# A gated recurrence on one core: the unbounded gathers of the first four tiles bring two layers of gates instead of one

## The chip, the cores and the metric

The kernel runs on one core of one Trainium2 chip. The metric is the device time of one execution in microseconds (us). The engines are PE (TensorE), DVE (VectorE), ACT (ScalarE), POOL (GpSimd) and SP (SyncE, which here only issues DMAs).

## The reference

2048 rows of 256 numbers pass six layers. In each, the row's token picks one row of a gate table with 4000 rows:

```python
def _L0_rec_ref(state, token, ih, hh):
    n_layers = ih.shape[0]                 # 6
    for i in range(n_layers):
        gate = ih[i][token]                # ih: 6 x 4000 x 256
        state = jnp.tanh(state + jnp.matmul(state, hh[i]) * gate)   # hh: 6 x 256 x 256
    return state
```

The tokens are drawn from 49 to 31985, so about seven in eight lie beyond the table, and for them the last row of the table is what the reference reads. All is float32.

## The kernel before

**Tiling.** The 2048 rows are 16 tiles of 128, taken in 8 pairs q. `order` lists 48 steps (layer, pair), all pairs of layer 0 first, then all of layer 1, and so on; every engine runs a program written out by hand in this order, and semaphores tie the engines together.

**One step.** PE multiplies the pair's state (as columns) by the layer's weights: in layer 0 in float32 (line 288), in later layers as three float16 products of a head and a rest (line 296). DVE multiplies the product by the gates into `sums` (`gated`, lines 465 and 468); the old state is added by DVE (line 480, all of layer 0) or POOL (line 280); ACT takes the tanh (line 403). For the next layer the new state has to be split and turned: for even pairs PE turns it (line 328), then ACT and DVE make head and rest (lines 385 and 485); for odd pairs ACT and DVE make head and rest of the rows (lines 391 and 492) and SP issues a DMA transpose (line 233). In layer 0 the old rows of pairs 1 to 7 come from PE too (line 336). Weights are scaled by powers of two that come out of column sums (`w_sums`, `totals` at line 345, `scales`); the totals for layers 2 to 5 stand in PE's program right after the first product of layer 1 and wait for the last addition of layer 0.

**Gates.** `gates` holds, for every tile, six layers of 256 numbers for each of its 128 rows. POOL fills it by indirect DMAs, one after another (the gathers), in two ways:

- For tiles 0 to 3 (`FIRST`), an unbounded gather brings layer 0 alone from `gate_first`, a table whose last row stands 128 times so that all tokens beyond the end find one (line 263). It waits for nothing but the index.
- A bounded gather skips the indices beyond the table. Its destination is filled beforehand with the table's last row, by an ACT or DVE copy from `last_rows` (`fill`, lines 367 and 430). Tiles 4 to 15 get all six layers in this way (line 273), then tiles 0 to 3 get layers 1 to 5 from `gate_later` (line 270).

POOL issues the four unbounded gathers, then the bounded ones of tiles 4 to 15, then those of tiles 0 to 3. `first_in[q]` and `gates_in[q]` count what has landed. DVE waits for `first_in` (q 0 and 1) or `gates_in` (q 2 to 7) ahead of the gating in layer 0, and for `gates_in` of q 0 and 1 ahead of their gating in layer 1.

**Loads.** SP loads the token, `last_rows` (768 KB), then for each pair the state's columns (line 204, 256 KB) and, between them, the weights of each layer (line 211, 256 KB) and the rows of pair 0 (line 208). From pair 2 on a load waits until the load two pairs earlier has landed.

Of the kernel before, what the change touches and what calls it, by code (L numbers as in the profile page):

```python
# [5 lines left out]
def gated_recurrence(nc, token, state_cols, state_rows, weights, gate_first, gate_later, gate_rows, gate_last, out):  # L6
# [18 lines left out]
    PAIR = 2  # L25
    PAIRS = TILES // PAIR
    LAST = LAYERS - 1
    SPLIT = LAYERS - 1

    order = [(l, q) for l in range(LAYERS) for q in range(PAIRS)]  # L30
# [4 lines left out]

    DMA_PAIRS = (1, 3, 5, 7)
    PE_INSTEAD = ()

    TURN_LAG = 3
    HEAD_LAG, HEAD_ROWS_LAG = 3, 1  # L40
# [6 lines left out]


    FIRST = (0, 1, 2, 3)
    GATHERS = (4, 5, 6, 7, 8, 9, 10, 11, 12, 13, 14, 15, 0, 1, 2, 3)  # L50
    ACT_FILLS = {-1: (5, 7, 10, 12, 14, 0, 1), 1: (2,)}
    DVE_FILLS = {-1: (4, 6, 8, 9, 11, 13), 0: (15,), 2: (3,)}
# [21 lines left out]
    PRODUCTS, TURNED, COPIES = 3, 2, 2  # L74

    def by_dma(i):
        return order[i][0] < LAST and order[i][1] in DMA_PAIRS and order[i] not in PE_INSTEAD

    def by_pe(i):
        return order[i][0] < LAST and not by_dma(i)  # L80
# [25 lines left out]
    with ExitStack() as ctx:  # L106
        def sb(name, shape, dt):
            return ctx.enter_context(nc.sbuf_tensor(name, shape, dt))
# [4 lines left out]
        def sem(name):  # L113
            return ctx.enter_context(nc.semaphore(name))
# [5 lines left out]
        gates = sb("gates", [P, TILES, LAYERS, HID], fp32)  # L120
# [32 lines left out]
        first_in = [sem(f"first_in{q}") for q in range(PAIRS)]  # L153
# [28 lines left out]
        def pair_rows(t, q):  # L182
            return t[:, PAIR * q:PAIR * (q + 1), :]
# [63 lines left out]
        @block.gpsimd  # L247
        def _(pool):
            nc.gpsimd.iota(limit[:, :], pattern=[[0, 1]], base=VOCAB - 1, channel_multiplier=1).then_inc(limit_ready, 1)
            nc.gpsimd.memset(ident[:, :], 0.0).then_inc(ident_zero, 1)  # L250
            pool.wait_ge(ident_zero, 1)
            nc.gpsimd.affine_select(out=ident[:, :], in_=ident[:, :], compare_op=ALU.not_equal, fill=1.0,
                                    base=0, pattern=[[-1, P]], channel_multiplier=1).then_inc(ident_ready, 1)

            pool.wait_ge(index_steps, INDEX_STEPS)
            by_act = [t for tiles in ACT_FILLS.values() for t in tiles]
            by_vector = [t for tiles in DVE_FILLS.values() for t in tiles]

            def offset(t):
                return bass.IndirectOffsetOnAxis(ap=index[:, t:t + 1], axis=0)  # L260

            for t in FIRST:
                pool.indirect_dma_start(gates[:, t, 0, :], None, gate_first, offset(t)).then_inc(first_in[t // PAIR], 16)  # L263
            for t in GATHERS:
                if t in by_act:
                    pool.wait_ge(act_filled, by_act.index(t) + 1)
                else:
                    pool.wait_ge(vector_filled, by_vector.index(t) + 1)
                if t in FIRST:
                    pool.indirect_dma_start(gates[:, t, 1:, :].rearrange("p l h -> p (l h)"), None, gate_later, offset(t),  # L270
                                            bounds_check=VOCAB - 1, oob_is_err=False).then_inc(gates_in[t // PAIR], 16)
                else:
                    pool.indirect_dma_start(gates[:, t].rearrange("p l h -> p (l h)"), None, gate_rows, offset(t),  # L273
                                            bounds_check=VOCAB - 1, oob_is_err=False).then_inc(gates_in[t // PAIR], 16)

            for i in range(STEPS):
                if on_pool(i):
                    q = order[i][1]
                    pool.wait_ge(gated_ready, i + 1)
                    nc.gpsimd.tensor_tensor(sums[:, q], sums[:, q], pair_rows(state, q),  # L280
                                            ALU.add).then_inc(pool_added, 1)
# [80 lines left out]
        @block.scalar  # L362
        def _(act):
            def fill(t):
                act.wait_ge(last_in, 16)
                lo = 1 if t in FIRST else 0
                nc.scalar.activation(gates[:, t, lo:, :].rearrange("p l h -> p (l h)"), last_rows[:, lo * HID:],  # L367
                                     ACT.Copy).then_inc(act_filled, 1)

            def w_sums(l):  # L370
                act.wait_ge(w_in[1 + l], 16)
                if l >= 1:
                    act.wait_ge(w_sum_ready, l)
                nc.scalar.activation(w_abs[:, :], w_full[:, 1 + l, :], ACT.Abs,
                                     accum_out=w_sum[:, l:l + 1]).then_inc(w_sum_ready, 1)

            def w_make_head(l):
                act.wait_ge(scale_steps, (1 if l == 0 else 2) * SCALE_STEPS)
                nc.scalar.activation(w_head[:, l, :], w_full[:, 1 + l, :], ACT.Copy,  # L379
                                     scale=w_up[:, :].bitcast(fp32)[:, l:l + 1]).then_inc(w_head_ready, 1)  # L380

            def make_head(i):
                q = order[i][1]
                act.wait_ge(turned_ready, pe_turns(i))
                nc.scalar.activation(split_cols[:, q, 0], turned_bank(i)[:, :, :, :], ACT.Copy,  # L385
                                     scale=STATE_SCALE).then_inc(head_ready, 1)

            def make_head_rows(i):
                q = order[i][1]
                act.wait_ge(copy_ready, dma_turns(i))  # L390
                nc.scalar.activation(split_rows[:, q, 0], copy_bank(i)[:, :, :], ACT.Copy,  # L391
                                     scale=STATE_SCALE).then_inc(head_rows_ready, 1)

            def new_state(i):
                q = order[i][1]
                if on_pool(i):
                    act.wait_ge(pool_added, pool_adds(i))
                else:
                    act.wait_ge(vector_added, vector_adds(i))
                for n, cut in enumerate(cuts(i)):  # L400
                    if n >= 1:
                        act.wait_ge(vector_added, vector_adds(i) + n)
                    nc.scalar.activation(pair_rows(state, q)[:, cut], sums[:, q, cut], ACT.Tanh).then_inc(state_ready, 1)  # L403
                if by_dma(i):
                    if dma_turns(i) > COPIES:
                        act.wait_ge(rest_rows_ready, dma_turns(i) - COPIES)
                    nc.scalar.activation(copy_bank(i)[:, :, :], sums[:, q], ACT.Tanh).then_inc(copy_ready, 1)  # L407

            for t in ACT_FILLS[-1]:
                fill(t)  # L410
            for i in range(STEPS):
                if i >= HEAD_LAG and by_pe(i - HEAD_LAG):
                    make_head(i - HEAD_LAG)
                if i >= HEAD_ROWS_LAG and by_dma(i - HEAD_ROWS_LAG):
                    make_head_rows(i - HEAD_ROWS_LAG)
                new_state(i)
                for t in ACT_FILLS.get(i, ()):
                    fill(t)
                if i in SUMS_AT:
                    w_sums(SUMS_AT[i])  # L420
                if i in HEADS_AT:
                    w_make_head(HEADS_AT[i])
# [3 lines left out]
        def _(dve):  # L426
            def fill(t):
                dve.wait_ge(last_in, 16)
                lo = 1 if t in FIRST else 0
                nc.vector.tensor_copy(gates[:, t, lo:, :].rearrange("p l h -> p (l h)"),  # L430
                                      last_rows[:, lo * HID:]).then_inc(vector_filled, 1)

# [22 lines left out]
            def gated(i, n, cut):  # L455
                layer, q = order[i]
                dve.wait_ge(product_ready, i + 1 + n)
                if layer == 0:
                    dve.wait_ge(first_in[q] if PAIR * q in FIRST else gates_in[q], 16 * PAIR)
                elif layer == 1 and PAIR * q in FIRST:  # L460
                    dve.wait_ge(gates_in[q], 16 * PAIR)
                product = product_bank(i, cut)[:, cut]
                g = pair_rows(gates, q)[:, cut, layer, :]
                if layer == 0:
                    nc.vector.tensor_tensor(sums[:, q, cut], product, g, ALU.mult).then_inc(gated_ready, 1)  # L465
                else:
                    down = w_down[:, :].bitcast(fp32)[:, layer - 1:layer]
                    nc.vector.scalar_tensor_tensor(out=sums[:, q, cut], in0=product, scalar=down, in1=g,  # L468
                                                   op0=ALU.mult, op1=ALU.mult).then_inc(gated_ready, 1)
# [96 lines left out]
```

## Time and profile before

| | us |
|---|---|
| median of 3 runs | 102.38 (102.11 to 102.92) |
| the profiled execution | 102.9 |
| its span in the trace | 101.1 |
| PE / DVE / ACT / POOL busy | 86.9 / 80.1 / 77.5 / 68.2 |

The span is what the engines' records cover; 1.8 us of the profiled execution lie around it. A busy share is an average over a load stage with layer 0, a dense middle and a tail, whose limits differ. Times in the trace count from the span's start.

### The profile page before, as it was taken

The page shows a single profiled execution, that of the slowest core. Times are in us where ns is not written, and L with a number is a line of the kernel's source. Part 1 is how long each engine was busy: PE and PEld are TensorE (multiplying, and loading weights), DVE is VectorE, ACT ScalarE, POOL GpSimd, SP SyncE. Part 2 cuts the span into 40 slices and gives each one's busy share as a digit, 9 for nine tenths or more (in the row PEclk, how much of TensorE's full clock was granted, in tenths as well). Part 3 has the DMA queues.
Part 4 walks back from the last instruction along what each step waited for, and adds up shares of the span by engine and source line. Part 5 has one row for each costly group of instructions (what it writes and reads, how often), then busy time and mean ns, then how long its engine had stood idle before and what let it go on. Part 6 is the DMA issues. An engine that isn't in the chain of part 4 may idle for free.

```text
span 101.1 us, 1829 instructions
## 1 busy us (share of the span) xinstructions
PE 86.9 (86%) x664; PEld 76.0 (75%) x664; DVE 80.1 (79%) x128; ACT 77.5 (77%) x133; POOL 68.2 (67%) x63
## 2 busy tenths in 40 slices
PE   5209999969995299999999999999999999999910
PEld 5108588948883277999999999999999999988800
DVE  1159966697660775789999899998999999989990
ACT  5059999799871266789699998999989978992641
POOL 3578787777772045477698868987499949879000
PEclk9999999999999655999999999999999999999995
DMA  1899899953999405057255551544545425964984
GB/s 23 286 338 392 258 280 314 334 186 96 70 107 169 53 3 110 0 104 59 52 104 102 104 104 35 112 82 90 104 60 121 81 55 104 96 118 82 367 310 174
DMA packets 27368, 14.25 MB, mean 141 GB/s; under 512 B 23772, under 2 KB 24028, under 8 KB 27360
## 3 DMA queue, kind: packets, MB, share of 16 engines
q1 hardware_dynamic: 24864, 12.07, 52.1%
q0 software_dynamic: 2496, 2.07, 10.1%
q8 instruction: 5, 0.08, 0.3%
q14 instruction: 3, 0.02, 0.1%
HBM read 17.31 MB, written 2.10 MB: 192 GB/s over the span
## 4 chain that ended last, share of the span: by engine, by line
PE 55%; DVE 17%; DMA 13%; issue 7%; POOL 6%; ACT 0%; SPq 0%; DVEq 0%; POOLq 0%
PE products L296 46%; DMA gates<-in_gate_rows,index 8%; PE turned L328 8%; DVE gates L430 6%; POOL gates L273 6%; DMA last_rows<-in_gate_last 5%; DVE sums L468 4%; DVE sums L480 4%; DVE split_cols L485 1%; DVE sums L465 1%; DVE split_rows L492 1%; PE spare L345 1%; ACT state L403 0%; SPq L225 0%; POOLq L273 0%
## 5 line engine op out<-in xcount | busy, mean ns | idle before, releaser
L296 PE MATMUL products<-w_head,split_cols 128*128 128x256 f16 x316 | 57.1, 279 | 0.0
L280 POOL TENSOR_TENSOR sums<-sums,state 128x512 f32<-128x512 f32 x36 | 45.6, 1272 | 16.9 <-DVE sums L468 16.5
L296 PE MATMUL products<-w_rest,split_cols 128*128 128x256 f16 x158 | 44.1, 279 | 0.0
L403 ACT ACTIVATE state<-sums 128x512 f32<-128x512 f32 (+1 forms) x49 | 30.4, 619 | 15.2 <-DVE sums L480 7.3
L296 PEld LDWEIGHTS products<-w_head,split_cols 128*128 128x128 f16 x316 | 31.9, 101 | 4.0
L468 DVE SCALAR_TENSOR_TENSOR sums<-products,w_down,gates 128x512 f32<-128x512 f32 (+1 forms) x40 | 29.5, 738 | 4.8 <-PE products L296 4.8
L288 PE MATMUL products<-w_full,first_cols 128*128 128x256 f32 x64 | 18.0, 430 | 4.6 <-DMA w_full<-in_weights 4.4
L288 PEld LDWEIGHTS products<-w_full,first_cols 128*128 128x128 f32 x64 | 13.3, 218 | 7.4 <-issue 4.7
L296 PEld LDWEIGHTS products<-w_rest,split_cols 128*128 128x128 f16 x158 | 15.8, 100 | 2.1
L273 POOL DMA_INDIRECT gates<-in_gate_rows,index x12 | 13.2, 1097 | 3.7 <-issue 3.4
L367 ACT ACTIVATE gates<-last_rows 128x1536 f32<-128x1536 f32 (+1 forms) x8 | 10.6, 1390 | 4.1 <-DMA last_rows<-in_gate_last 4.1
L485 DVE SCALAR_TENSOR_TENSOR split_cols<-turned,split_cols 128x512 f16<-128x512 f32 x20 | 13.6, 679 | 0.0
L492 DVE SCALAR_TENSOR_TENSOR split_rows<-copies,split_rows 128x512 f16<-128x512 f32 x20 | 13.6, 679 | 0.0
L328 PE MATMUL turned<-ident,state 128*128 128x128 f32 x80 | 12.5, 280 | 0.0
L391 ACT ACTIVATE split_rows<-copies 128x512 f16<-128x512 f32 x20 | 11.8, 590 | 0.4
L385 ACT ACTIVATE split_cols<-turned 128x512 f16<-128x512 f32 x20 | 11.7, 585 | 0.1
L407 ACT ACTIVATE copies<-sums 128x512 f32<-128x512 f32 x20 | 11.7, 587 | 0.0
L465 DVE TENSOR_TENSOR sums<-products,gates 128x512 f32<-128x512 f32 x8 | 5.5, 688 | 6.4 <-DMA gates<-in_gate_rows,index 4.2
L328 PEld LDWEIGHTS turned<-ident,state 128*128 128x128 f32 x80 | 9.9, 146 | 0.4
L430 DVE COPY gates<-last_rows 128x1536 f32<-128x1536 f32 (+1 forms) x8 | 7.2, 946 | 3.1 <-DMA last_rows<-in_gate_last 3.1
L451 DVE SCALAR_TENSOR_TENSOR w_rest<-w_full,w_up,w_head 128x512 f16<-128x512 f32 x5 | 6.3, 1257 | 0.8 <-ACT w_head L379 0.8
L263 POOL DMA_INDIRECT gates<-in_gate_first,index x4 | 4.7, 1178 | 2.6 <-DVE index L507 1.7
(37 smaller groups left out, 40.0 us busy)
## 6 DMA issues: line engine op xcount, KB each, us to landing
first_cols<-in_state_cols SPq DMA_DIRECT2D x8, 256.0 KB, 4.1
out<-state SPq DMA_DIRECT2D x7, 256.0 KB, 2.4
w_full<-in_weights SPq DMA_DIRECT2D x6, 256.0 KB, 5.4
last_rows<-in_gate_last SPq DMA_DIRECT2D x1, 768.0 KB, 4.9
split_cols<-split_rows SPq DMA_TRANSPOSE x20, 3.0
state<-in_state_rows SPq DMA_DIRECT2D x1, 256.0 KB, 6.2
out<-state SPq DMA_DIRECT2D x2, 128.0 KB, 1.7
gates<-in_gate_rows,index POOLq DMA_INDIRECT x12, 4.8
```

The lines of the kernel that those rows point to most:

```text
L273: pool.indirect_dma_start(gates[:, t].rearrange("p l h -> p (l h)"), None, gate_rows, offset(t), bounds_check=VOCAB - 1, oob_is_err=False) ...
L280: nc.gpsimd.tensor_tensor(sums[:, q], sums[:, q], pair_rows(state, q), ALU.add).then_inc(pool_added, 1)
L288: last = nc.tensor.matmul(bank[:, j, :], first_cols[:, q, k, j * P:(j + 1) * P], w_full[:, 0, k * HID:(k + 1) * HID], start=(k == 0), stop ...
L296: last = nc.tensor.matmul(bank[:, j, :], split_cols[:, q, s, j, k, :], w[:, l - 1, k * HID:(k + 1) * HID], start=(n == 0), stop=(n == len( ...
L328: last = nc.tensor.transpose(turned_bank(i)[:, j, k, :], state[:, PAIR * q + j, k * P:(k + 1) * P], ident[:, :])
L385: nc.scalar.activation(split_cols[:, q, 0], turned_bank(i)[:, :, :, :], ACT.Copy, scale=STATE_SCALE).then_inc(head_ready, 1)
L391: nc.scalar.activation(split_rows[:, q, 0], copy_bank(i)[:, :, :], ACT.Copy, scale=STATE_SCALE).then_inc(head_rows_ready, 1)
L403: nc.scalar.activation(pair_rows(state, q)[:, cut], sums[:, q, cut], ACT.Tanh).then_inc(state_ready, 1)
L430: nc.vector.tensor_copy(gates[:, t, lo:, :].rearrange("p l h -> p (l h)"), last_rows[:, lo * HID:]).then_inc(vector_filled, 1)
L468: nc.vector.scalar_tensor_tensor(out=sums[:, q, cut], in0=product, scalar=down, in1=g, op0=ALU.mult, op1=ALU.mult).then_inc(gated_ready, 1)
L485: nc.vector.scalar_tensor_tensor(out=split_cols[:, q, 1], in0=turned_bank(i)[:, :, :, :], scalar=STATE_SCALE, in1=split_cols[:, q, 0], op0 ...
L492: nc.vector.scalar_tensor_tensor(out=split_rows[:, q, 1], in0=copy_bank(i)[:, :, :], scalar=STATE_SCALE, in1=split_rows[:, q, 0], op0=ALU. ...
```

## The change

The unbounded gathers of tiles 0 to 3 bring layers 0 and 1, 2 KB a row instead of 1 KB, from a `gate_first` of twice the width. The fills and the bounded gathers of these four tiles begin at layer 2, four layers instead of five. DVE waits for the bounded gathers of q 0 and 1 ahead of layer 2 instead of layer 1. `DMA_INSTEAD` is an empty tuple, so the new `by_dma` picks the same steps as before.

```diff
@@ FIRST
     FIRST = (0, 1, 2, 3)
+    FIRST_LAYERS = 2
@@ by_dma
-        return order[i][0] < LAST and order[i][1] in DMA_PAIRS and order[i] not in PE_INSTEAD
+        layer, q = order[i]
+        return layer < LAST and (q in DMA_PAIRS and (layer, q) not in PE_INSTEAD or (layer, q) in DMA_INSTEAD)
@@ POOL
             for t in FIRST:
-                pool.indirect_dma_start(gates[:, t, 0, :], None, gate_first, offset(t)).then_inc(first_in[t // PAIR], 16)
+                pool.indirect_dma_start(gates[:, t, :FIRST_LAYERS, :].rearrange("p l h -> p (l h)"), None, gate_first,
+                                        offset(t)).then_inc(first_in[t // PAIR], 16)
...
                 if t in FIRST:
-                    pool.indirect_dma_start(gates[:, t, 1:, :].rearrange("p l h -> p (l h)"), None, gate_later, offset(t),
+                    pool.indirect_dma_start(gates[:, t, FIRST_LAYERS:, :].rearrange("p l h -> p (l h)"), None, gate_later, offset(t),
                                             bounds_check=VOCAB - 1, oob_is_err=False).then_inc(gates_in[t // PAIR], 16)
@@ fill, on ACT and on DVE
-                lo = 1 if t in FIRST else 0
+                lo = FIRST_LAYERS if t in FIRST else 0
@@ gated, on DVE
-                elif layer == 1 and PAIR * q in FIRST:
+                elif layer == FIRST_LAYERS and PAIR * q in FIRST:
                     dve.wait_ge(gates_in[q], 16 * PAIR)
@@ host
-    gate_first = _np.concatenate([gate_rows[:, :hid], _np.repeat(gate_rows[-1:, :hid], 127, axis=0)])
+    gate_first = _np.concatenate([gate_rows[:, :2 * hid], _np.repeat(gate_rows[-1:, :2 * hid], 127, axis=0)])
...
-        "gate_later": gate_rows[:, hid:],
+        "gate_later": gate_rows[:, 2 * hid:],
```

No instruction changes its place on its engine; what changes is the wait on two of DVE's. Here is DVE's program from the last gating of layer 0 to the second of layer 1, before:

```order
L465 TENSOR_TENSOR sums<-products,gates 128x512 [waits gates_in7,product_ready]
L485 SCALAR_TENSOR_TENSOR split_cols<-turned,split_cols 128x512 [waits head_ready]
L480 TENSOR_TENSOR sums<-sums,spare 128x512 [waits rows_turned,gated_ready]
L437 TENSOR_SCALAR w_total<-spare 128x4 [waits total_ready]
L440 TENSOR_SCALAR w_expo<-w_total 128x4 [waits scale_steps]
L443 TENSOR_SCALAR w_up<-w_expo 128x4 [waits scale_steps]
L446 TENSOR_SCALAR w_down<-w_expo 128x4
L468 SCALAR_TENSOR_TENSOR sums<-products,w_down,gates 128x512 [waits gates_in0,product_ready]
L492 SCALAR_TENSOR_TENSOR split_rows<-copies,split_rows 128x512 [waits head_rows_ready]
L468 SCALAR_TENSOR_TENSOR sums<-products,w_down,gates 128x512 [waits gates_in1,product_ready]
```

And the same stretch of DVE after the change:

```order
L469 TENSOR_TENSOR sums<-products,gates 128x512 [waits gates_in7,product_ready]
L489 SCALAR_TENSOR_TENSOR split_cols<-turned,split_cols 128x512 [waits head_ready]
L484 TENSOR_TENSOR sums<-sums,spare 128x512 [waits rows_turned,gated_ready]
L441 TENSOR_SCALAR w_total<-spare 128x4 [waits total_ready]
L444 TENSOR_SCALAR w_expo<-w_total 128x4 [waits scale_steps]
L447 TENSOR_SCALAR w_up<-w_expo 128x4 [waits scale_steps]
L450 TENSOR_SCALAR w_down<-w_expo 128x4
L472 SCALAR_TENSOR_TENSOR sums<-products,w_down,gates 128x512 [waits product_ready]
L496 SCALAR_TENSOR_TENSOR split_rows<-copies,split_rows 128x512 [waits head_rows_ready]
L472 SCALAR_TENSOR_TENSOR sums<-products,w_down,gates 128x512 [waits product_ready]
```

The waits for `gates_in0` and `gates_in1` have moved eight steps down, to the first two gatings of layer 2; that for `gates_in7`, the last of layer 0, stays.

## Rows read from the trace of the kernel before

**Rows 1.** The chain that ended last: start us, us, what:
```profile
24.74 7.93 DMA gates<-in_gate_rows,index
...
34.69 0.59 PE spare L345 x2
35.28 2.58 PE products L296 x12
37.87 0.85 PE turned L328 x4
38.72 3.59 PE products L296 x24
42.31 0.44 PE turned L328 x4
42.75 2.62 PE products L296 x24
...
88.60 1.32 PE products L296 x12
```

**Rows 2.** DVE in order of time: start us, us, what, idle before and releaser:
```profile
11.34 0.68 DVE L465 TENSOR_TENSOR sums<-products,gates 128x512 f32<-128x512 f32 x1
...
14.39 0.69 DVE L465 TENSOR_TENSOR sums<-products,gates 128x512 f32<-128x512 f32 x1 [0.78 <-PE products L288]
...
17.89 0.89 DVE L430 COPY gates<-last_rows 128x1280 f32<-128x1280 f32 x1
...
32.76 0.69 DVE L465 TENSOR_TENSOR sums<-products,gates 128x512 f32<-128x512 f32 x1 [3.34 <-DMA gates<-in_gate_rows,index]
...
35.88 0.74 DVE L468 SCALAR_TENSOR_TENSOR sums<-products,w_down,gates 128x512 f32<-128x512 f32 x1
...
37.90 0.75 DVE L468 SCALAR_TENSOR_TENSOR sums<-products,w_down,gates 128x512 f32<-128x512 f32 x1 [0.68 <-PE products L296]
```

**Rows 3.** Waits from 0 to 36 us: total us, times, longest:
```profile
PE spare L345 <- DVE sums L480: 3.0, 1, 3.0
...
PE spare L336 <- DVE sums L480: 0.9, 1, 0.9
...
PE products L288 <- DMA first_cols<-in_state_cols: 0.2, 1, 0.2
```

**Rows 4.** The page's 40 slices of the span (2.53 us each), granted clock in tenths:
```profile
PEclk9999999999999655999999999999999999999995
```

**Rows 5.** POOL in order of time:
```profile
7.48 1.44 POOL L263 DMA_INDIRECT gates<-in_gate_first,index  x1 [0.30 <-issue]
...
17.93 0.99 POOL L273 DMA_INDIRECT gates<-in_gate_rows,index  x1 [0.30 <-issue]
...
27.33 0.99 POOL L270 DMA_INDIRECT gates<-in_gate_later,index  x1 [0.30 <-issue]
...
29.93 0.99 POOL L270 DMA_INDIRECT gates<-in_gate_later,index  x1 [0.30 <-issue]
```

**Rows 6.** DMA, us to landing: the gathers issued at 27.33 and at 29.93:
```profile
gates<-in_gate_later,index POOLq DMA_INDIRECT x1, 6.3
...
gates<-in_gate_later,index POOLq DMA_INDIRECT x1, 4.7
```

**Rows 7.** Stretches of 2 us: stretch, PE, PEld, DVE, ACT, POOL busy, clock, DMA share, GB/s:
```profile
8.00:10.00 2.00, 2.00 (x6) 1.55 (x6) 2.00 (x3) 2.00 (x2) 1.70 (x2) 1.00 1.05 406
10.00:12.00 2.00, 1.78 (x5) 0.97 (x4) 2.00 (x3) 2.00 (x3) 1.70 (x2) 1.00 0.95 307
...
22.00:24.00 2.00, 1.64 (x10) 1.52 (x11) 2.00 (x4) 1.96 (x5) 1.55 (x2) 1.00 0.30 80
```

**Rows 8.** Groups by line and form, 0 to 36 us: busy us, mean ns, idle before:
```profile
L367 ACT ACTIVATE gates<-last_rows 128x1280 f32<-128x1280 f32 x3 | 3.7, 1255 | 0.0
```

**Rows 9.** DMA transposes, us to landing: the one issued at 23.5 us, then the median of all:
```profile
split_cols<-split_rows SPq DMA_TRANSPOSE x1, 8.9
...
split_cols<-split_rows SPq DMA_TRANSPOSE x20, 3.0
```

More of the change, by code:

```diff
@@ L37, in gated_recurrence @@
     PE_INSTEAD = ()
+    DMA_INSTEAD = ()
     TURN_LAG = 3
@@ L428, in fill @@
                 dve.wait_ge(last_in, 16)
-                lo = 1 if t in FIRST else 0
+                lo = FIRST_LAYERS if t in FIRST else 0
                 nc.vector.tensor_copy(gates[:, t, lo:, :].rearrange("p l h -> p (l h)"),
```

## The prediction

> **What bounds the kernel now.** I read the chain of waits first. From 34.69 us to the last product at 88.60 it is nothing but PE: 24 products of 2.62 us and a turn of 0.44 us, over and over [rows 1]. Nothing that frees DVE, ACT or POOL there gives time. Ahead of that block stands one transfer: the gather issued at 24.74, in flight for 7.93 us, landed at 32.66 [rows 1]. It is the twelfth bounded gather, tile 15, and the order of POOL's program says so: four unbounded ones, then tiles 4 to 15. DVE's program shows who needs it. The last gating of layer 0, pair 7, starts at 32.76 after 3.34 us of idleness that this gather ended [rows 2]. Its addition releases the totals at line 345, for which PE sat idle 3.0 us [rows 3]. So layer 0 ends when tile 15's gates land, and all else in layer 0 has some 3 us to spare.
>
> The idleness costs a second time. The granted clock falls from full to half (2.4 to 1.2 GHz) in slices 14 to 16, roughly 33 to 40 us [rows 4], behind the 3.0 us in which PE did nothing. Twelve products, a turn and 24 products take 2.58 + 0.85 + 3.59 = 7.02 us there; at the later rate they are 1.32 + 0.44 + 2.62 = 4.38 us [rows 1]. The low clock costs 2.6 us.
>
> The question is therefore narrow: does the change move the landing of tile 15's gates, or the idleness of PE before it?
>
> **The wait that is taken out.** The gatings of pairs 0 and 1 in layer 1 no longer wait for the bounded gathers of tiles 0 to 3. These were issued at 27.33 (tile 1, the last of pair 0) and 29.93 (tile 3, the last of pair 1) [rows 5] and needed 6.3 and 4.7 us to land [rows 6]: 33.6 and 34.6. The gatings started at 35.88, straight behind the scales, and at 37.90, after 0.68 us of waiting for PE's products [rows 2]. Both gathers were there 2.3 and 3.3 us earlier. The removed wait was worth nothing: 0 us. It would only be worth something if the rest of layer 0 ended over 2 us earlier, and it ends on tile 15, whose gather stands ahead of these in the same queue.
>
> **The bytes that are added.** Each unbounded gather brings 128 rows of 1 KB more; four of them 4 x 128 x 1024 = 0.52 MB. They fall where the DMA engines are full: 406 GB/s at a share of 1.05 from 8 to 10 us, 307 GB/s at 0.95 from 10 to 12 us [rows 7]. The extra transfer takes 0.52 MB / 406 = 1.3 us to 0.52 / 307 = 1.7 us of all engines. Three things can be late by up to that.
>
> - The first gating at 11.34, which waits for pair 0's unbounded gathers. The second one, at 14.39, had 0.78 us of idleness ahead [rows 2] that takes up most of it.
> - The columns of pair 1, for which PE waited 0.2 us [rows 3] ahead of its second product. They are in flight beside the gathers, so this wait grows by something between 0 and 1.3 us; I take the middle, some 0.7 us, as loads and gathers share the engines. PE has 0.9 us of idleness later in layer 0, ahead of a line 336 [rows 3], and 3.0 us at its end.
> - The gathers queued behind: tiles 4 to 15. The engines catch up, at a share of 0.30 and 80 GB/s from 22 to 24 us [rows 7]. The gathers issued from then on, tiles 14 and 15 among them, find nothing left of the early load.
>
> All of this is covered by the wait for tile 15, with 3.0 us of cover. Without that cover it would be 0.7 us on the path, at most 1.7. So: 0 us, bounds 0 to +1.7.
>
> **What is taken off the fills and the late gathers.** ACT's fills of tiles 0, 1 and 2 shrink from 1280 to 1024 columns. One of 1280 takes 1255 ns [rows 8], so each gives back up to 1255 x 256/1280 = 0.25 us: 0.5 us ahead of ACT's first tanh, another 0.25 us in layer 0. DVE's fill of tile 3 at 17.89, 0.89 us [rows 2], gives back about 0.89 x 256/1280 = 0.18 us. All of it lies in layer 0, under the same cover: 0 us. Without the cover it would offset half a microsecond of the delay above. The late gathers bring about an eighth of their rows, one layer less: 4 x 128 x 1024 / 8 = 0.07 MB, 0.2 us of the engines by the rates above, all behind tile 15 in its queue: 0 us.
>
> **POOL.** Its issues, not its transfers, pace the gathers: 0.99 us and 0.30 us between, whether a row is 6 KB or 5 KB [rows 5]. I take the same for 2 KB rows in place of 1 KB. The bound is from both sides: the fourth unbounded issue took 1.44 us beside DVE's copies [rows 5], and should the doubled rows cost four issues a tenth more each, tile 15 is issued 0.4 us later; they might as well be 0.4 us cheaper. The row that is nearest, 5 against 6 KB with no difference, says 0.
>
> The issue at 17.93 took 0.99 us although it lay wholly beside the DVE copy at 17.89 [rows 2, 5]. The Trainium skill's page "SBUF — State Buffer" says otherwise of such a copy (section "SBUF: two separate sides", on DVE blocking a DMA from GpSimd): a float32 copy from SBUF to SBUF locks GpSimd out of the port that it writes descriptors through. By that rule the shorter fill would let POOL go on up to 0.18 us sooner and the time would be 0.2 us lower; by the row it gains nothing. The 1.44 us at 7.48 agrees with the page, this row does not, and the sum does not rest on it.
>
> **What stays uncertain: why tile 15 took 7.93 us.** The first DMA transpose, issued at 23.5, needed 8.9 us where the median of all 20 is 3.0 [rows 9]. It was in flight together with the gathers of tiles 13 to 15, and both kinds were slow. If layer 0 runs 0.7 us later up to pair 4, this transpose is issued 0.7 us later, for it waits for DVE's rest of pair 1. Tile 15 was issued 1.2 us behind it, so the two still meet. Taking the meeting as it was, tile 15 lands at 32.7 again. The bounds are wide: if the knot moves with the transpose, 33.4 to 34.4; if an earlier gather slips out ahead of it, 31 or less.
>
> **The sum.** Wait removed 0, added bytes 0, fills 0, POOL 0, knot 0: the profiled execution would stay at 102.9 us, with a span of 101.1, and the median of the runs, which is 0.5 us below that execution, at 102.4 us. Its own range is 101.4 to 103.4, the 1% that a measurement of this kernel can tell from no change.
>
> **Rival 1, slower: the knot moves with the load.** The 1.3 to 1.7 us of extra transfer push back pair 1's columns, the products, DVE's rest of pair 1, and so the first transpose; tile 15's gates, tied up with it, land 1.3 us later, at 34.0. It decides from the point where tile 15 lands after 32.7. PE restarts 1.3 us later, and the time is 102.4 + 1.3 = 103.7, with 1.7 us 104.1. For it: both transfers were slow together [rows 1, 9]. Against it: the tile is issued at a fixed 24.74, and the load has slack of 0.78 and 0.9 us on the way.
>
> **Rival 2, faster: the clock holds.** PE's work of layer 0 ends later by 0.7 us while tile 15 lands as before, so PE idles 2.3 us instead of 3.0. The one fall of the clock in the middle came behind an idleness of 3.0 us [rows 3, 4]; the trace has no idleness of 2 us there to say whether that would do. If the clock stays full, 2.6 us go: 99.8.
>
> **Rival 3, faster: the gathers slip past the transpose.** With the first transpose later, tiles 13 and 14 land before it and tile 15 meets less. If it lands 1.5 us earlier the time is 100.9; if it took 4.7 us, like the gather issued at 29.93 [rows 6], PE's idleness of 3.0 and the low clock's 2.6 would both go, 96.8. The transpose is only moved by 0.7 us against a stretch of some 8, which speaks against it.
>
> **How the numbers follow.** No change: 0.50. Rival 1: 0.20, and another 0.05 for still slower (a longer low clock, or dearer issues on POOL). Rival 2: 0.14. Rival 3: 0.11, nearly all of it near 100.9. The range takes in rival 1 up to 104.1 and rival 2 down to 99.6, which leaves out about 0.12. Faster by over 1%: 0.25; within 1%: 0.50; slower by over 1%: 0.25.
>
> **What the changed profile would show.** The first gating up to 1 us later than 11.34; PE's wait for the columns of pair 1 longer than 0.2 us; POOL's issues of the twelve ending at about 25.7 again; DVE's longest wait of layer 0 still for tile 15, ended near 32.7; no wait for the late gathers in either layer 1 or 2; PE's idleness ahead of line 345 between 2 and 3 us, and the clock at half behind it. The forecast is wrong if tile 15 lands more than 1 us away from 32.7, or if the clock does not fall.

## The result, and the profile after

| | before, us | changed, us |
|---|---|---|
| median | 102.65 (102.11 to 103.91, 4 runs) | 106.12 (104.82 to 106.55, 4 runs) |
| ratio | | 1.026, 95% interval 1.014 to 1.039 |
| profiled execution | 102.9 | 106.46 |
| its span | 101.1 | 104.7 |

Only one of the four runs of the kernel before, the one at 103.91, was taken beside the changed kernel; the other three are those of the table ahead of the prediction. The ratio leaves out the changed kernel's two slower runs (106.46 and 106.55); that of the two medians is 1.034. The runs below show that this matters: the same kernel before has medians from 98.3 to 106.9 us in different sets of runs.

The page of the changed kernel: its span, the granted clock and the DMA share in 40 slices of 2.62 us, and two rows of its last part, the DMAs with their time to landing.

```profile
span 104.7 us, 1829 instructions
PEclk9999999999955559999999999999999999999998
DMA  1999989964931050055935433555505555663985
first_cols<-in_state_cols SPq DMA_DIRECT2D x8, 256.0 KB, 5.1
gates<-in_gate_rows,index POOLq DMA_INDIRECT x12
```

The last row has no time to landing, though it had one (4.8 us) before: this trace lacks many of the events that tell when a DMA landed. What an engine waited for is then put down to "remote" or to whatever came last. The clock is at half for four slices, where three were lowered before [rows 4].

The chain that ended last (start, us, what), where layer 0 ends:

```profile
4.35 7.58 DMA first_cols<-in_state_cols
...
25.31 1.62 another core or an unknown queue
...
28.43 4.19 PE products L292 x8
...
35.69 3.41 PE products L292 x8
39.10 0.50 PE turned L332 x4
39.61 0.44 PE spare L340 x4
40.05 1.31 PE products L300 x12
41.35 0.12 PE spare L349 x2
...
92.15 1.32 PE products L300 x12
```

Line 349, the totals behind layer 0, comes at 41.35 us instead of 34.69 [rows 1]: 6.7 us later. From there to the last product it is 50.8 us, against 53.9 before, which began at half clock. 6.7 less 3.1 is the 3.6 us that the span grew. So all of the loss lies ahead of the totals, in layer 0.

But it isn't tile 15 that ends it. DVE and ACT in order of time:

```profile
24.02 0.69 DVE L469 TENSOR_TENSOR sums<-products,gates 128x512 f32<-128x512 f32 x1 [2.06 <-remote]
27.03 0.69 DVE L484 TENSOR_TENSOR sums<-sums,spare 128x512 f32<-128x512 f32 x1 [1.71 <-remote]
...
28.80 0.19 ACT L378 ACTIVATION_READ_ACCUMULATOR w_abs<-w_full 128x1 f32 x1
...
32.64 0.69 DVE L469 TENSOR_TENSOR sums<-products,gates 128x512 f32<-128x512 f32 x1 [4.92 <-PE products L292]
32.70 0.60 ACT L389 ACTIVATE split_cols<-turned 128x512 f16<-128x512 f32 x1 [3.70 <-remote]
```

The gating at 32.64 is that of pair 5, the sixth. It waits for PE's product and for the gates of tiles 10 and 11, whose landing this trace doesn't tell. ACT's head of pair 2 at 32.70 waits for nothing but PE's turn of that pair, and this is what PE did:

```profile
24.25 0.60 PE L332 MATMUL turned<-ident,state 128*128 128x128 f32 x4
27.77 0.66 PE L340 MATMUL spare<-ident,first_cols 128*128 128x128 f32 x4 [2.92 <-DVE sums L484]
```

The turn was over at 24.85, and ACT had been idle since 29.0. It waited 3.7 us for a signal that by the record was long given, and it and DVE went on within 0.06 us of each other. The last of POOL's gathers was issued at 29.76. I call this the stall of layer 0. Nothing of the kind stands in the trace before.

### The profile page after: what moved, and what is told of

It reads as the page before. It is cut to its first block, busy times and chain, and to the rows that moved or that the text cites. A ratio compares the mean times of both kernels' runs of the same rounds, so it can differ in the third digit from the quotient of the medians.

```text
span 104.7 us, 1829 instructions
## 1 busy us (share of the span) xinstructions
PE 86.7 (83%) x664; PEld 75.8 (72%) x664; DVE 80.1 (77%) x128; ACT 76.6 (73%) x133; POOL 68.0 (65%) x63
## 4 chain that ended last, share of the span: by engine, by line
PE 65%; DVE 14%; DMA 7%; another core or an unknown queue 4%; issue 3%; SPq 3%; ACT 0%; DVEq 0%
PE products L300 44%; PE products L292 11%; PE turned L332 8%; DMA first_cols<-in_state_cols 7%; DVE sums L484 5%; DVE sums L472 4%; PE spare L340 3%; DVE sums L469 2%; SPq L214 2%; DVE split_rows L496 1%; DVE split_cols L489 1%; DVE gates L434 1%; SPq L211 0%; SPq L207 0%
## 5 line engine op out<-in xcount | busy, mean ns | idle before, releaser
L300 PE MATMUL products<-w_head,split_cols 128*128 128x256 f16 x316 | 54.8, 273 | 0.0
L300 PE MATMUL products<-w_rest,split_cols 128*128 128x256 f16 x158 | 43.1, 273 | 0.0
L300 PEld LDWEIGHTS products<-w_head,split_cols 128*128 128x128 f16 x316 | 31.0, 98 | 3.4
L292 PE MATMUL products<-w_full,first_cols 128*128 128x256 f32 x64 | 20.0, 468 | 5.1 <-DMA w_full<-in_weights 4.5
L292 PEld LDWEIGHTS products<-w_full,first_cols 128*128 128x128 f32 x64 | 14.3, 235 | 8.3 <-issue 4.7
L371 ACT ACTIVATE gates<-last_rows 128x1536 f32<-128x1536 f32 (+1 forms) x8 | 9.9, 1310 | 4.0 <-DMA last_rows<-in_gate_last 4.0
L395 ACT ACTIVATE split_rows<-copies 128x512 f16<-128x512 f32 x20 | 11.8, 590 | 0.4
L411 ACT ACTIVATE copies<-sums 128x512 f32<-128x512 f32 x20 | 11.8, 588 | 0.0
L340 PE MATMUL spare<-ident,first_cols 128*128 128x128 f32 x28 | 4.8, 300 | 7.1 <-DVE sums L484 6.2
L340 PEld LDWEIGHTS spare<-ident,first_cols 128*128 128x128 f32 x28 | 3.5, 151 | 8.7 <-DVE sums L484 7.2
```

The costliest lines, as they stand in the source:

```text
L292: last = nc.tensor.matmul(bank[:, j, :], first_cols[:, q, k, j * P:(j + 1) * P], w_full[:, 0, k * HID:(k + 1) * HID], start=(k == 0), stop ...
L300: last = nc.tensor.matmul(bank[:, j, :], split_cols[:, q, s, j, k, :], w[:, l - 1, k * HID:(k + 1) * HID], start=(n == 0), stop=(n == len( ...
```

## The experiments

They came in five sets; the runs of one set share a chip and the runs of the kernel before. Means, since medians of six leave much spread:

| set | before (repeats of it included) | changed | difference |
|---|---|---|---|
| 1 | 106.40 (24 runs) | 108.02 (6) | +1.6 |
| 2 | 105.91 (11) | not run | |
| 3 | 98.09 (11) | 99.42 (6) | +1.3 |
| 4 | 105.83 (17) | 106.83 (6) | +1.0 |
| 5 | 98.58 (29) | 98.73 (6) | +0.2 |

**Set 1: the kernels again, and each half of the change alone.** The first two are the kernel before and the changed kernel, with no edit.

> The kernel before, unchanged, to see how its own time and its wait for tile 15 repeat. Theory A (the 0.52 MB of extra gates slow the load and layer 0): 102 to 103 us, the chain again through tile 15, the clock falling once. Rival B (the stalls of 1.7 to 4.9 us on DVE and ACT that the changed kernel's trace shows without a releaser belong to an execution, not to a kernel): some of them show here too, with times up to 104 or more.

106.9 us (106.05 to 108.66), and 105.8 for the set's 18 other runs of it: ratio of a kernel to itself 1.017, interval 1.007 to 1.026 (1.009 by the means of all runs). The interval thus understates what runs of one kernel differ by. Its trace has the stall, on DVE and on ACT:

```profile
27.62 0.69 DVE L480 TENSOR_TENSOR sums<-sums,spare 128x512 f32<-128x512 f32 x1 [1.71 <-remote]
33.27 0.69 DVE L465 TENSOR_TENSOR sums<-products,gates 128x512 f32<-128x512 f32 x1 [4.97 <-PE products L288]
...
33.33 0.60 ACT L385 ACTIVATE split_cols<-turned 128x512 f16<-128x512 f32 x1 [3.75 <-remote]
```

These are nearly the changed kernel's rows, 0.6 us later. Rival B holds: the stall isn't the change's.

> The changed kernel, unchanged. Theory A: 105 to 106 us in most executions, ratio 1.02 to 1.04, layer 0 ending 5 us later than before. Rival B: a ratio of 1.00 to 1.02 with a wide interval, and a trace without the stalls.

107.98 us (106.84 to 109.69), ratio 1.025 (1.016 to 1.034), the stall up to 33.08. Against all 24 runs of before it is +1.6 us.

```diff
# bytes only, against before
-pool.indirect_dma_start(gates[:, t, 0, :], None, gate_first, offset(t))
+pool.indirect_dma_start(sums[:, 4 + t].rearrange("p l h -> p (l h)"), None, gate_first, offset(t))
...
+if layer == 0 and PAIR * q in FIRST:
+    g = sums[:, 4 + PAIR * q:4 + PAIR * (q + 1), 0, :][:, cut]
...
```

> The kernel before, whose unbounded gathers bring two layers a row (2 KB) into the unused sums of pairs 4 to 7, of which layer 0 alone is read; fills, bounded gathers and waits as before. Theory A (bytes): as slow as the changed kernel, 105 to 106 us. Rival C (the shorter fills, the narrower late gathers or the moved wait do it): 102.4 us. Rival B: anything from 102 to 106.

107.03 us (105.06 to 109.69), mean 107.24, +0.8 on before.

```diff
# narrow only, against the changed kernel
-pool.indirect_dma_start(gates[:, t, :FIRST_LAYERS, :].rearrange("p l h -> p (l h)"), None, gate_first, offset(t))
+pool.indirect_dma_start(gates[:, t, 0, :], None, gate_first, offset(t))
...
-g = pair_rows(gates, q)[:, cut, layer, :]
+g = pair_rows(gates, q)[:, cut, 0 if layer == 1 and PAIR * q in FIRST else layer, :]
...
```

> The changed kernel with the unbounded gathers bringing layer 0 alone, as before; layer 1 of pairs 0 and 1 is gated with layer 0's gates, so the gates of layer 1 are left out for these tiles. Fills, late gathers and wait as changed. Theory A: 102.4 us or a little less, as before. Rival C: 105 to 106 us.

105.9 us (102.26 to 108.8, 12 runs), mean 105.71, -0.7. The signs fit theory A rather than rival C, but the sizes lie within the spread of 1.0 to 1.8 us (standard deviation of the runs of one kernel in this set).

**Set 2: what holds up layer 0.** Before 106.03 us (100.93 to 109.61, 11 runs).

```diff
-GATHERS = (4, 5, 6, 7, 8, 9, 10, 11, 12, 13, 14, 15, 0, 1, 2, 3)
+GATHERS = (4, 5, 6, 7, 8, 9, 10, 11, 12, 13, 14, 15)
...
```

DVE's waits for these gathers in layer 1 became one wait for ACT's fills.

> The kernel before without the four bounded gathers of tiles 0 to 3; their gates of layers 1 to 5 stay the table's last row, so this part of the gating is left out for tokens inside the table. Theory D (as long as GpSimd's gathers are in flight, signals between the engines come late, and DVE and ACT go on only when the last gather is through, near 33 us): both go on at about 28 us, and the kernel is 3 to 5 us faster, 101 to 102 where before is 106. Rival E (DVE waits for gates of its own pair, which the trace lost): nothing that DVE waits for in layer 0 is changed, so within 1 us of before.

98.64 us (96.68 to 99.21): 7.4 us faster, more than expected, and what the kernel before takes in the sets without the stall below (98.3 and 98.5). This trace lacks landing events too, so their loss doesn't by itself go with longer times. The last wait without a releaser on DVE ended at 27.59, and the clock never fell:

```profile
27.59 0.69 DVE L480 TENSOR_TENSOR sums<-sums,spare 128x512 f32<-128x512 f32 x1 [1.59 <-remote]
```

```diff
# eight late gathers: layers 1 to 3, then, for all four tiles, layers 4 and 5
-pool.indirect_dma_start(gates[:, t, 1:, :].rearrange("p l h -> p (l h)"), None, gate_later, offset(t), ...)
+pool.indirect_dma_start(gates[:, t, 1:4, :].rearrange("p l h -> p (l h)"), None, gate_later, offset(t), ...)
...
+for t in FIRST:
+    pool.indirect_dma_start(gates[:, t, 4:, :].rearrange("p l h -> p (l h)"), None, gate_last_two, offset(t), ...)
...
```

> The kernel before with the late gathers of tiles 0 to 3 cut in two, layers 1 to 3 and, behind them all, layers 4 and 5: four gathers more, the same bytes, 128 rows each. The gating of layer 1 in pairs 0 and 1 waits for both. Theory D: DVE and ACT go on at about 38 us instead of 33, the kernel 3 to 5 us slower. Rival E: layer 0 ends as before, the time within 1 us of before, since layer 1 begins at 41 us anyhow.

111.44 us (107.65 to 111.93): 5.4 us slower, for as many bytes. POOL's last issue and DVE's last long wait:

```profile
35.76 1.00 POOL L277 DMA_INDIRECT gates<-in_gate_last_two,index  x1 [0.30 <-issue]
...
38.25 0.69 DVE L484 TENSOR_TENSOR sums<-sums,spare 128x512 f32<-128x512 f32 x1 [2.35 <-remote]
```

With 20 gathers (the changed kernel's first trace) and with 24, DVE's last wait of this kind ends 2.9 us (29.76 to 32.64) and 2.5 us (35.76 to 38.25) behind the start of the last issue. In all eleven traces of sets 1, 2 and 4 and of the first comparison that have the stall and 20 gathers, before and changed alike, it ends between 32.6 and 33.5 us. With 16 gathers no such wait comes that late. The one that is left there, 1.59 us at 27.59, doesn't follow the last gather: with 20 gathers the kernel before had one of 1.71 us at 27.62 in set 1, and here tile 15, the last gather, landed at 29.3, after DVE had gone on.

So theory D's forecasts came out in direction, by more than its 3 to 5 us, and rival E's, within 1 us of before, in neither run: the late end of layer 0 hangs on the late gathers. That any gather in flight holds the engines up is not shown.

> The kernel before with all 16 bounded gathers made unbounded ones of 1 KB a row from the short table (layer 0, and layer 1 for the last four): as many gathers, about as many bytes, but no row skipped. Gates of the other layers are left out for tokens inside the table. Theory D in its narrower form (the skipped rows, seven in eight, each a packet of 4 bytes, delay the signals): no stalls on DVE and ACT without a releaser, no lost events, 3 to 5 us faster. If the gathers as such do it, no change.

Edit: both bounded forms became `indirect_dma_start(gates[:, t, 0 or 1, :], None, gate_first, offset(t))`. 106.42 us (105.73 to 107.57), and DVE's long wait, here of 4.93 us ahead of pair 4's gating, ended at 32.96. So it isn't the skipped rows; theory D's narrower form falls.

> The changed kernel with four layers instead of two in the unbounded gathers, 4 KB a row: 1.05 MB more than the change and 1.57 MB more than before; fills and late gathers bring layers 4 and 5 alone. Theory A (each 0.52 MB costs 1 to 1.7 us of the load that layer 0 can't hide): 3 to 5 us slower than before. If the load has the slack that the prediction gave it: within 1 us of before.

Edit: `FIRST_LAYERS = 4` and a table to match. 105.89 us (102.25 to 106.92), no slower than before: where the stall ends layer 0, 1.57 MB more cost nothing that shows. Theory A falls for this set. In its trace PE's second product began at 13.65 us, later than in most.

**Set 3: versions with fewer or later gathers.** Here before ran at 98.26 us (97.12 to 98.98), and the traces, none of them of the kernel before, have their landing events and no stall. So these runs can't test theory D.

```diff
# late gathers in layer 1, against the changed kernel
-GATHERS = (4, 5, 6, 7, 8, 9, 10, 11, 12, 13, 14, 15, 0, 1, 2, 3)
+GATHERS = (4, 5, 6, 7, 8, 9, 10, 11, 12, 13, 14, 15)
+LATE_AT = {8: 0, 9: 1, 10: 2, 11: 3}
...
                                             ALU.add).then_inc(pool_added, 1)
+                if i in LATE_AT:
+                    gather(LATE_AT[i])
```

> The changed kernel, whose four late gathers POOL issues behind its additions of steps 8 to 11 in layer 1, one behind each, in place of ahead of layer 0's end; nothing is left out, since layer 2 is the first to need them. Theory D (gathers in flight hold up the other engines): layer 0 ends as in the run without late gathers, the wait ends near 28 us, 98 to 101 us in all; if they hold up layer 1 instead, up to 104. If the late gathers were innocent: as the changed kernel, 106 to 108.

102.25 us (100.72 to 104.35), ratio 1.037. POOL's additions are pushed apart by the gathers:

```profile
38.89 1.29 POOL L287 TENSOR_TENSOR sums<-sums,state 128x512 f32<-128x512 f32 x1
40.34 1.00 POOL L275 DMA_INDIRECT gates<-in_gate_later,index  x1 [0.16 <-issue]
41.36 1.28 POOL L287 TENSOR_TENSOR sums<-sums,state 128x512 f32<-128x512 f32 x1
```

And PE now waits in layer 1, by the waits from 34 to 60 us (total, times, longest):

```profile
ACT state L412 <- POOL sums L287: 4.7, 5, 1.3
...
PE turned L337 <- ACT state L412: 2.8, 2, 1.9
```

> The changed kernel with all six layers in the unbounded gathers of tiles 0 to 3, so that their fills and the four late gathers are gone: 16 gathers instead of 20, nothing left out, but 2.6 MB more than before in the load. Theory D with little cost of bytes: 99 to 102 us. Theory A (1 to 1.7 us for each 0.52 MB): 5 to 8 us of load on top, 103 to 107.

Edit: `FIRST_LAYERS = 6`, tiles 0 to 3 out of `GATHERS` and of the fills. 102.47 us (102.31 to 102.58), ratio 1.046. Its waits name the cost:

```profile
DVE sums L469 <- DMA gates<-in_gate_first,index: 6.9, 2, 4.6
...
PE products L292 <- DMA first_cols<-in_state_cols: 5.3, 1, 5.3
```

PE waits 5.3 us for the columns of pair 1, where it waited 0.2 before [rows 3]. Without a stall behind it, 2.6 MB cost 4.4 us (mean to mean), 1.7 us for each MB, although four gathers and their fills are gone.

> The changed kernel once more, beside the kernel before on this chip. If the change costs something of its own: a ratio of 1.015 to 1.03 again. If the first comparison and the second were mostly the spread of layer 0 from one execution to the next: 0.99 to 1.01.

99.35 us (96.53 to 102.10), +1.3 on before by the means. The profiled execution, the slowest of the six, has tile 15 in flight for 8.1 us, landed at 33.0, and two slices of lowered clock: the picture of [rows 1, 4].

> Unbounded gathers for tiles 0 and 1 alone, all six layers; tiles 2 to 15 by bounded gathers: 16 gathers, nothing left out, 1.2 MB more than before instead of 2.6. Theory D: 98 to 101 us, at least as fast as the one with four tiles.

Edit: the same with `FIRST = (0, 1)` and tiles 2 and 3 bounded ahead of tile 4. 101.11 us (100.87 to 101.98), ratio 1.034: 3.2 us by the means for 1.2 MB, so the cost isn't simply in proportion to the bytes. No version beats the kernel before where it runs without the stall.

**Set 4: both kernels and both halves once more.** It fell into the stall again (before 106.83 us; one of its 11 runs, at 100.54 us with the clock full throughout, looks free of it but has no trace).

> The kernel before, for a trace beside the others of this call. If its 98.3 us of the last call is a layer 0 without a wait for tile 15: PE goes from layer 0 to layer 1 without a gap, the clock doesn't fall there, span 96.5. If the wait is there, 101 to 103 us.

> The changed kernel. Theory F (where no wait for tile 15 covers it, the later columns of pair 1 are on the path; where it does, they are not): 0.5 to 1.5 us slower than before in this call. The prediction's theory (covered): within 0.5 us of before.

> The kernel before with 2 KB a row in the unbounded gathers, the second KB unused. Theory F: as the changed kernel or slower by up to 0.3 us, as it has the longer fills; second product of PE at 12 to 13.7 us.

> The changed kernel with 1 KB a row in the unbounded gathers, the gates of layer 1 in pairs 0 and 1 left out for those of layer 0. Theory F: as before or up to 0.5 us faster, second product of PE near 11.5 us.

Medians 105.63, 106.67, 106.22 and 106.80; means 105.84, 106.83, 105.79 and 105.84. Only the whole change stands above the others, by 1.0 us, with runs of one kernel spread by 0.9 to 2.1 us (standard deviation), and neither half shows a cost. PE's second product began at 11.9, 12.7, 12.8 and 11.4 us.

**Set 5: before and changed kernel without the stall.**

> The kernel before once more. If this call is like the third (before at 98 us): its trace has all events, no stall without a releaser, and shows whether PE waits for tile 15. Otherwise 105 to 107 us with the stalls again.

98.40 us (96.41 to 103.48, 12 runs; 98.54 in the set's 17 others). The chain of waits into layer 1:

```profile
24.58 6.15 DMA gates<-in_gate_rows,index
...
32.76 0.39 PE spare L345 x2
33.15 1.33 PE products L296 x12
```

Tile 15 took 6.15 us instead of 7.93 [rows 1] and landed at 30.73, the totals came at 32.76, and the clock held.

> The changed kernel once more. Theory F: slower than before by 0.5 to 1.5 us where before is at 98, by less than 1 us where it is at 106.

99.25 us (97.01 to 99.90), mean 98.73, +0.2. Theory F asked for 0.5 to 1.5 us where before is at 98; with an uncertainty of 0.6 us this doesn't decide it. The chain no longer goes through tile 15:

```profile
4.19 7.81 DMA first_cols<-in_state_cols
12.01 4.79 DMA first_cols<-in_state_cols
16.80 0.04 issue
16.84 1.99 PE products L292 x8
...
30.53 1.31 PE products L300 x12
31.84 0.18 PE spare L349 x2
```

The columns set the pace of layer 0, and its end is PE's own work at 31.84. Tile 15's gather took 4.0 us, from 25.05 to 29.07, and the first DMA transpose 5.2 us, where the prediction's trace had 7.93 and 8.9 [rows 1, 9]. The span of 95.2 us is the shortest of all traces, and it is one of the changed kernel.

## Why the prediction was wrong

**The removed wait, 0 us: right.** No trace of the kernel before has DVE wait for a late gather in layer 1. In the one after, the gating of layer 1 starts at 42.07 behind the scales, as before.

**The added bytes: the delay right and somewhat larger, the cover not what I took it for.** PE's second product started at 11.4 to 12.5 us in nine traces with 1 KB a row (mean 11.8) and at 12.0 to 13.8 in eight with 2 KB (mean 12.9): 1.1 us later, where I took 0.7 within 0 to 1.3. With the stall behind it, three times these bytes cost nothing; without it and with no late gathers, 2.6 MB cost 4.4 us. The cover of 3.0 us that I counted on was the wait for tile 15 in one execution. In the last trace of the changed kernel it wasn't there at all.

**The fills and the late gathers, 0 us: not told apart.** Set 1 gives -0.7 us for them, set 4 gives 0.0.

**POOL, 0 us: right.** The last bounded issue of tiles 4 to 15 started at 24.59, against 24.74 [rows 1]. The doubled rows cost no issue time, and the shorter fill on DVE, now at 17.56, changed nothing that shows.

**Tile 15 and the clock: right that they are uncertain, wrong that one row stands for them.** In the complete traces of the two kernels it landed at 32.66 and 30.73 before, at 33.0 and 29.07 after the change; the clock fell in the two where it landed near 33. Its gather and the first transpose were slow or fast together, as the prediction read it: 7.93 and 8.9 us, 6.15 and 6.3, 8.12 and 9.2, 4.0 and 5.2. In the three complete traces where no late gathers stood behind it in layer 0, tile 15 took 3.6 to 5.2 us; whether these gathers slow it was not tested further. Rivals 1, 2 and 3 are the spread of either kernel rather than effects of the change: rival 2's and 3's times, 99.8 and 96.8, are what the kernel before itself reaches. The changed kernel's execution in set 3 that looks like [rows 1, 4] took 102.1 us against the 102.9 that the prediction gave for such a one: within that picture its account holds.

**The step that failed is the sum's last one:** "the profiled execution would stay at 102.9 us [...] and the median of the runs [...] at 102.4 us". It took one execution of the kernel before as its time, and with it the path of that execution, "layer 0 ends when tile 15's gates land, and all else in layer 0 has some 3 us to spare". In the changed kernel's trace the path was another: a wait of 4.92 us ahead of pair 5's gating, for which the sum has no term, and the totals 6.7 us later. The kernel has two ways through layer 0, with the stall near 106 us and without it near 98 (102.9 in the profiled execution, where tile 15 was late; its other runs, at 102.1 to 103.9, have no trace). The changed kernel was traced with the stall, the kernel before without it. The range ended at 104.1, and a range that held both would have reached past 107.

**What the change costs by itself** is the difference within a set: +1.6, +1.3, +1.0 and +0.2 us, 1.0 us on average with an uncertainty of some 0.4 (the spread of the four, 0.6, by the root of 4, and a bit for the runs' own). That is 1%, at the edge of what I called no change, not the 2.6% of the first comparison. The largest, in set 1, stands beside two groups of the kernel before itself that differ by 1.0 us (107.12 and 106.16). The rest of the 3.5 us between the first medians goes with the stall, which the changed kernel's trace has and the trace before doesn't.

**What stays open:** by what path the late gathers hold up signals between other engines, and why most runs of some sets have it and others don't; one chip showed both. The stall came in all 13 traces that lack landing events (in the one without late gathers it was short) and in none of the 7 that have them, so the two may have one cause, or the recording may cause the stall. But the run without late gathers lost events and had the times of a kernel without the stall. I had no run without recording. Loading of instructions is not the cause: in both traces of set 4 of the kernels themselves no instruction queue moved anything from 20 to 35 us, and the stall is there.

## What to carry to other kernels

Ahead of a comparison, run the kernel before against itself in the same set: here that gave 1.017, and a kernel's runs from another set are no baseline at all (98.3 and 106.8 us for one kernel on one chip). A wait in one trace is a cover only if other executions have it too. When engines wait for signals that the record says are given, look for what is in flight at that time, and take some of it away or double it: four gathers less or more moved this kernel by -7.4 and +5.4 us, while three times the disputed bytes did nothing.

## What the runs showed of the hardware

- In 13 traces, while GpSimd's gathers were being issued or in flight, DVE waited 1.6 us and more for signals recorded as given; in 8 of them ACT waited 2.3 to 4.4 us for a turn of PE that was over. With 20 gathers the last such wait of DVE ended at 32.6 to 33.5 us, with 24 at 38.25; with 16 none came after 27.59.
- Whether seven in eight rows of a gather are skipped or none made no difference that shows (106.4 against 106.0 us, runs spread by 2 us).
- The gather of tile 15 took 4.0 to 8.1 us to land in the four complete traces of the two kernels, and the first DMA transpose beside it 5.2 to 9.2 us, slow and fast together.
